# Self-attention's loop reordered: maxima spread over four scores, a reciprocal in two halves, on one core

## The reference

```python
scale = 1.0 / jnp.sqrt(jnp.asarray(D_K, dtype=jnp.float32))      # D_K = 64
q = jnp.einsum('bsd,hdk->bhsk', x, w_q)
k = jnp.einsum('bsd,hdk->bhsk', x, w_k)
v = jnp.einsum('bsd,hdk->bhsk', x, w_v)
scores = jnp.einsum('bhqk,bhmk->bhqm', q, k) * scale
weights = jax.nn.softmax(scores, axis=-1)
z = jnp.einsum('bhqm,bhmk->bhqk', weights, v)
z = jnp.transpose(z, (0, 2, 1, 3)).reshape(b, s, h * dk)
return x + jnp.einsum('bse,ed->bsd', z, w_o)
```

## Time and profile before

| what | us |
|---|---|
| time, median of 3 runs | 689.75 |
| lowest and highest run | 688.6, 691.35 |
| time of the profiled execution | 690.05 |
| span of its instructions | 688.3 |
| PE, DVE, ACT, POOL busy | 613.8, 446.1, 289.7, 245.6 |
| self-attention's loop, 16 pairs | from 240.9 to 474.4 |
| one pair without a slot (i = 2 to 9) | 13.79 |

### The profile page before, as it was taken

How to read it: one execution, slowest core, us unless ns; L and a number is a source line. 1 busy time by engine, 2 the same in 40 slices (tenths; PEclk the granted TensorE clock), 3 DMA queues, 4 the chain that set the end, 5 groups by cost and what they waited for, 6 DMA issues and landing times.

```text
span 688.3 us, 8792 instructions
## 1 busy us (share of the span) xinstructions
PE 613.8 (89%) x3171; PEld 309.4 (45%) x3172; DVE 446.1 (65%) x1168; ACT 289.7 (42%) x552; POOL 245.6 (36%) x178
## 2 busy tenths in 40 slices
PE   7875769999897899999999988999598999999995
PEld 4422457976652322222223422235332446665655
DVE  6899997457669557766676578676645763333334
ACT  7979967032312564444444334443053351212110
POOL 2898452232501544465446335555160100000001
PEclk9957979999998999999999999999799999999998
DMA  8200023030000000000000000004200000000001
GB/s 316 98 0 0 2 90 158 1 123 1 1 1 0 0 1 0 1 0 1 1 1 1 1 0 0 1 1 159 101 1 0 1 0 1 0 1 1 0 1 31
DMA packets 3681, 18.92 MB, mean 27 GB/s; under 512 B 917, under 2 KB 2198, under 8 KB 3126
## 3 DMA queue, kind: packets, MB, share of 16 engines
q1 hardware_dynamic: 3638, 18.36, 7.0%
HBM read 17.84 MB, written 0.52 MB: 27 GB/s over the span
## 4 chain that ended last, share of the span: by engine, by line
PE 65%; DVE 17%; ACT 8%; issue 5%; POOL 4%; POOLq 0%; DVEq 0%; ACTq 0%
PE PS L2356 11%; PE PS L1622 8%; PE PS L2370 7%; DVE SB L1851 6%; PE PS L1606 5%; PE PS L1564 5%; PE PS L1590 3%; PE PS L1636 2%; PE PS L1692 2%; DVE SB L199 2%; POOL SB L238 2%; DVE SB L212 2%; PE PS L2067 1%; ACT SB L468 1%; POOL SB L516 1%
## 5 line engine op out<-in xcount | busy, mean ns | idle before, releaser
L1837 POOL TENSOR_TENSOR SB<-SB 128x1024 f32<-128x1024 f32 x32 | 75.3, 2353 | 115.9 <-ACT SB L1789 115.0
L1851 DVE TENSOR_REDUCE SB<-PS 128x2 f32<-128x1024 f32 x64 | 78.4, 1225 | 56.6 <-PE PS L1590 56.5
L1789 ACT ACTIVATE SB<-PS 128x1024 f32<-128x1024 f32 x64 | 65.5, 1023 | 101.3 <-PE PS L1609 101.2
L2356 PE MATMUL PS<-SB 128*128 128x512 f32 x176 | 83.1, 609 | 0.0
L1606 PE MATMUL PS<-SB 64*128 64x512 f32 x256 | 69.0, 616 | 1.1 <-ACT SB L1793 1.1
L1622 PE MATMUL PS<-SB 128*64 128x512 f32 x256 | 67.7, 611 | 0.0
L2408 ACT ACTIVATE SB<-PS 128x512 f32<-128x512 f32 (+1 forms) x48 | 28.5, 595 | 90.4 <-PE PS L2356 87.6
L2433 DVE TENSOR_TENSOR SB<-SB,PS 128x512 f32<-128x512 f32 (+1 forms) x48 | 32.7, 687 | 48.1 <-PE PS L2356 43.7
L238 POOL TENSOR_TENSOR SB<-SB 128x4 f32<-128x4 f32 x18 | 19.3, 1072 | 119.6 <-DVE SB L204 119.5
L2370 PEld LDWEIGHTS PS<-SB 128*128 128x128 f32 (+1 forms) x384 | 50.8, 195 | 18.7 <-issue 10.5
L2370 PE MATMUL PS<-SB 128*128 128x128 f32 (+1 forms) x384 | 56.1, 291 | 1.4 <-DVE SB L2433 1.4
(11 more groups left out here) (403 smaller groups left out, 1127.1 us busy)
## 6 DMA issues: line engine op xcount, KB each, us to landing
SB<-exp SPq DMA_DIRECT2D x1, 4352.0 KB, 14.0
SB<-moe SPq DMA_DIRECT2D x1, 4096.0 KB, 14.2
SB<-dft SPq DMA_DIRECT2D x1, 2304.0 KB, 12.0
SB<-att SPq DMA_DIRECT2D x1, 2048.0 KB, 7.9
SB<-mix SPq DMA_DIRECT2D x1, 768.5 KB, 4.5
SB<-mix SPq DMA_DIRECT2D x1, 640.0 KB, 5.6
SB<-ssm SPq DMA_DIRECT2D x1, 602.0 KB, 6.6
SB<-lat SPq DMA_DIRECT2D x1, 585.0 KB
```

The costliest lines, as they stand in the source:

```text
L1789: act.activation(expd[i % 2][:, 1024 * u:1024 * u + 1024], bank(2 * (u % 2), 2), ACT.Exp).then_inc(sem("d_exp"), 1)
L1837: pool.tensor_tensor(half_sums[half], e[:, 0:1024], e[:, 1024:], ALU.add).then_inc(sem("d_half_sum"), 1)
L1851: dve.tensor_reduce(shift[i % 2][:, qt:qt + DK + 1:DK], two_heads(bank(4, 2)), AX_X, ALU.max, negate=True)\
L2356: pe.matmul(bank(2 * (i % 3) + side), exp_w["e_w13"][:, c:c + 128], xsT[:, 512 * n:512 * n + 512], start=True, stop=True).then_inc(sem(("t ...
```

## The change

Three things are reordered or cut. No matmul is added or removed.

- On PE, `maxima` 0 and 1 of the next pair stay where they are. `maxima` 2 moves from before `project(i + 2, 1)` to behind it, and `maxima` 3 moves from the end of step u = 1 to behind `score(i, 2)`.
- On PE, `sums(i - 1)` now comes ahead of `shifts(i + 1)`, which moves behind `weigh(i - 1, 2)`.
- On DVE, the reciprocal of bank 7 (128x512) is made in two halves of 256 columns. The first half is issued before `shift_in(i + 1)`, the second half where the whole was. `d_unit` is raised by the second half.

```diff
             for u in range(4):
                 score(i, u)
-                if ahead and u == 2:
-                    shifts(i + 1)
+                if ahead and u in (0, 2):
+                    maxima(i + 1, (0, 3)[u // 2])
                 if before and u == 2:
                     sums(i - 1)
-                if ahead and u < 2:
-                    maxima(i + 1, 2 * u)
                 if slot and u == 0:
                     beside(i)
                 elif i + 2 < NP_ and u < 2:
                     project(i + 2, u)
+                if ahead and u == 1:
+                    maxima(i + 1, 2)
                 if i == NP_ - 2 and u < 2:
                     context(u)
...
                 if slot and u == 0:
                     beside_read(i)
                     project(i + 2, 0)
-                if ahead and u < 2:
-                    maxima(i + 1, 2 * u + 1)
+                if ahead and u == 0:
+                    maxima(i + 1, 1)
+                if ahead and u == 2:
+                    shifts(i + 1)
...
-        def unit_of(i):
-            dve.wait_ge(sem("d_sums"), i + 1)
-            dve.reciprocal(unit, bank(7)).then_inc(sem("d_unit"), 1)
+        def unit_half(i, k):
+            if k == 0:
+                dve.wait_ge(sem("d_sums"), i + 1)
+            ins = dve.reciprocal(unit[:, 256 * k:256 * k + 256], bank(7)[:, 256 * k:256 * k + 256])
+            if k:
+                ins.then_inc(sem("d_unit"), 1)
+
+        def unit_of(i, halves=(0, 1)):
+            for k in halves:
+                unit_half(i, k)
             dve.wait_ge(sem("d_weighed"), i + 1)
             dve.wait_ge(sem("d_unit"), i + 1)
             dve.tensor_tensor(headed[:, 512 * i:512 * i + 512], heads_bank(i), unit, ALU.mult).then_inc(sem("d_headed"), 1)
...
                 maximum(i + 1, 2)
                 maximum(i + 1, 3)
+                if i >= 1:
+                    unit_half(i - 1, 0)
                 shift_in(i + 1)
...
             if i >= 1:
-                unit_of(i - 1)
+                unit_of(i - 1, (1,) if i + 1 < NP_ else (0, 1))
```

## The result

The changed kernel takes 683.92 us (median of 8 runs, 680.71 to 687.32), the kernel before 689.17 (8 runs, 687.85 to 691.76). The ratio is 0.9932, with a 95% interval from 0.9904 to 0.996. Two later series of the same kernel gave 0.9938 (0.9915 to 0.9961) and 0.9909 (0.9877 to 0.9941). The forecast was 682.6, in a range from 680.2 to 687.5. The profiled execution took 680.71, its span is 678.9. A few later executions, one of `edges` and some of the kernel before, took 741 us or more; they are left out of every number here.

A forecast was written before the change was run, and what follows sets the result against it. PE bounds the loop, losing 0.84 us a pair waiting for DVE. Terms -0.7 + 5.7 + 1.4 + 0.6 - 0.1 + 0.2 = 7.1 us take 690.05 to 682.95, less 0.3 to the median: 682.6, range 680.2 to 687.5.

The forecast's parts named there:

- The two waits: In the loop, PE idles for DVE's reduction ahead of a `maxima` and of `shifts`, 0.42 us each, 0.84 a pair.
- the distance rule of 1.72 us: Two `maxima` must start 1.72 us apart: DVE starts 0.43 behind one, takes 1.23, and PE follows 0.06 later.
- The new order's price: Start-to-start distances on PE sum to a pair of 13.22 us against 13.79; new neighbours take back 0.27 of 0.84.
- The second rival: Changes of matmul form on PE cost more: 0.27 us gained a pair instead of 0.57, time 686.2; chance 0.17.
- DVE's list: From `maxima` 3 on, reciprocal halves of 1.76 us and DVE's other work fit; thinnest slack 0.28 us, at `project`.
- The third rival: DVE becomes the chain: halves and starts cost 0.3 us more each, `project` waits 0.3 to 0.6 a pair, 688; chance 0.12.
- The fourth rival: A half reciprocal ahead of `shift_in` takes as long as the whole (3.36 us), delaying score 0 and `project`: about 720; chance 0.04.
- The pairs that differ: Loop edges: pair 0 loses 0.7 us, pair 11 gains 1.4, pair 12 0.57, pair 13 -0.08, pair 14 0.2, pair 15 nothing.
- The total: Whole loop: -0.7 + 5.7 + 1.4 + 0.6 - 0.1 + 0.2 = 7.1 us gained, giving 682.6 us.

The follow-up runs named there:

- edges: The changed kernel with pair 0 kept in the old order and, in pair 14, `maxima` 2 moved behind `context`: 683.08 us, ratio 0.9906.
- max2_alone: The kernel before with one move alone, `maxima` 2 behind `project` 1: 692.75 us in one execution, pairs of 13.85 us.
- weigh_early: `edges` with `weigh` 3 put directly behind `weigh` 2 in every pair but the last: 678.43 us, ratio 0.9844 against the kernel before.
- whole_behind: The changed kernel with the reciprocal whole (128x512) and behind `shift_in`, the new PE order kept: 688.23 us, ratio 0.9982.
- whole_ahead: The changed kernel with the reciprocal whole (128x512) and ahead of `shift_in`: 700.96 us, ratio 1.0199.
- sums_behind: The changed kernel with `sums` moved behind `weigh` 2, `shifts` still last: 695.46 us in one execution.
- after_again: The changed kernel run a second time with no edit: 683.01 us (6 runs); the profiled execution took 685.89.
- sums_behind_norm_first: `sums_behind` with `norm_apply` put ahead of the first half of the reciprocal in pairs 11 and 12: 685.1 us in one execution.
- old_order_halves: The kernel before, its PE order kept, with only the reciprocal in two halves, the first ahead of `shift_in`: 689.98 us, ratio 1.002.
- after_third: The changed kernel run a third time with no edit, beside `edges`: 683.11 us, ratio 0.9909.

## Why the prediction was right, point by point

- **The two waits.** Right: no idle time ahead of L1590 and L1597 in pairs 1 to 9, and the distance rule of 1.72 us came out to the hundredth in `max2_alone`. It is no gain for each move: the first alone gave -0.06, `shifts` in the wrong place gave 0.02. Only a whole pair in which every distance is over 1.72 gives anything.
- **The new order's price.** Right: 13.22 forecast, 13.24 measured. Reading distances from start to start, with one value for each pairing, is what made it exact; durations would have added up to more than the pair. The second rival (changes of form dearer) is refuted, and `weigh_early` shows the price from the other side.
- **DVE's list.** Right in its order, with slack understated: 0.28 forecast, 0.63 measured in the same count, because back-to-back DVE instructions overlap by 0.1 and `shift_in` took 0.63 and not 0.69. The third rival was refuted as the change stands, but `whole_behind` shows how near it lies: without the halves, `d_unit` comes too late and 0.41 of the 0.55 us a pair is gone.
- **The fourth rival** had two halves of 3.36 each. That didn't happen: they take 1.75. `whole_ahead` is the nearest case, with one such reciprocal ahead of `shift_in`. The mechanism is there (score 0 waits 0.79 us a pair for `shift_in`), and with L212 held and a stretch at clock 0.50 in pair 12 it costs 17 us.
- **The pairs that differ.** Pair 0 lost 0.73 (0.7), pair 11 gained 1.39 (1.4), pair 12 0.54 (0.57), pair 14 0.23 (0.2), and pair 13 neither gained nor lost (0.1 lost). In pair 12, L204 ended with POOL's sum again, as taken, and `maxima` 1 came 6.19 us behind score 0 as before (417.77 - 411.58, now 411.42 - 405.23):

```profile
409.07 1.16 DVE L204 TENSOR_SCALAR SB<-SB 128x4 f32<-128x4 f32 x1
```

  L204 ended at 410.23, and POOL's second sum, as its timeline has it, at 410.21:

```profile
405.43 2.35 POOL L1839 TENSOR_TENSOR SB<-SB 128x1024 f32<-128x1024 f32 x1 [5.00 <-ACT SB L1791]
407.86 2.35 POOL L1843 TENSOR_TENSOR SB<-SB 128x1024 f32<-128x1024 f32 x1
```

  In both pairs `beside` waits for `d_unit`, and the first `weigh` then for `d_headed`:

```profile
407.10 0.64 PE L1665 MATMUL PS<-SB 128*96 128x128 f32 x4 [0.32 <-DVE SB L1876]
...
422.98 0.66 PE L1999 MATMUL PS<-SB 128*128 128x128 f32 x4 [0.32 <-DVE SB L1876]
423.86 1.08 PE L1622 MATMUL PS<-SB 128*64 128x512 f32 x4 [0.23 <-DVE SB L1885]
```

  In pair 12 these waits cost nothing, since `maxima` 1 waits for DVE anyway. In pair 13 the total is right and its make-up isn't: the prediction had one wait of 0.65 for `d_unit`. Measured from start to start it is 0.39, the wait for `d_headed`, which it didn't have, is 0.30, and 0.13 came back at `project`. That the sum came out is luck.

- **What the prediction passed over.** The `norm_apply` in pair 11 of the changed kernel was over just as POOL's sum began (405.43, above):

```profile
404.28 1.10 DVE L212 TENSOR_SCALAR SB<-SB 128x128 f32<-128x128 f32 x4
```

  The end is 0.05 us ahead of the sum, but by `sums_behind` it is the starts that count. The last of the four starts at 405.04, 0.39 ahead of the sum; there one that started 0.16 ahead ran, and one that started 0.10 behind was caught. So the margin is between 0.23 and 0.49 us, and it is the same to 0.01 in pair 12 and in both other traces of this kernel. I had counted `norm_apply` at its 1.11 us without asking what POOL did then, so this term came out by luck. Had its last part been caught, it would have been held to the end of POOL's first sum, 407.78: an estimated 2 us at most in each of the two pairs, against a range that ended 3.6 above the median. No run shows just this case; in `sums_behind`, where two of the four were caught, it came to some 12 us with the clock.
- **The total.** 7.1 forecast, 6.86 in the loop, 5.25 in the medians. The forecast is 1.3 us off the measured median and not 1.9, because the kernel before came out at 689.17 this time and not at the 689.75 it started from: that is luck. The range held the difference between loop and total, the sum didn't contain it. A gain of 6.86 would be a ratio of 0.9900; the intervals of two of the three series leave it out (from 0.9904 and from 0.9915), the third holds it, so scatter alone is a weak reason. The mean granted clock of the changed kernel's executions was 0.950 in the first series and 0.954 in the two others, where the kernel before had 0.955. That fits more time at the lower clock outside the loop, but no run shows why there should be more, and the cause stays open.

## What to carry to other kernels

When one tile is shared between a producer and a consumer, write down the least distance between two uses (here 1.72 us) and lay out the producer's list so that every pair of uses is further apart; moving one use alone only moves the wait. Price a reordered PE list by distances from start to start for each pairing of neighbours, and keep work of one matmul form together. Before a `tensor_scalar` in SBUF is moved, or anything that moves it, look what POOL does at the new time, since being caught there cost more than the move could give.

## What the runs showed of the hardware

- A change of form between matmuls of 64 rows, 64 columns and the full array costs about 0.1 us behind the last pass (`maxima` 0.31 into another form, 0.23 into the same) and 0.05 to 0.1 in the first pass after it (`weigh` 1.01 against 0.96, a score's f32 part 0.96 against 0.85): two changes less gave 0.34 us a pair.
- DVE's reciprocals and `shift_in`, reading PSUM, start up to 0.1 us before the end of the instruction ahead (300.57 against 300.66 in the changed kernel), also across a wait that is already met.
- A `tensor_scalar` of 128x128 in SBUF takes 0.34 us by itself and took 2.37 and 2.49 under a POOL sum of 128x1024 (`sums_behind`), ending with it; two sums held back one each. Norm's statistics in SBUF and reductions from PSUM ran under such sums at their usual length (0.86, 0.38 and 1.23 in the changed kernel).
- The clock fell to 0.50 inside the loop nine times in the thirteen traces, for 3.4 us, or 6.8 in `sums_behind`; one stretch of 3.4 cost 1.66 us (`after_again`). Each began during an idle time of PE of 1.3 to 5.3 us or up to 1.3 us behind it: 1.32 in `after_again` and in `sums_behind_norm_first`, 1.86 to 2.38 in `max2_alone`, `old_order_halves` and `weigh_early`, 3.38 in `whole_ahead`, 5.25 in `sums_behind`. None fell into pairs 2 to 9, where PE has no such idle time. The same idle time often passed without one (1.32 in `after_third`); what decides that stayed open.
